# Moments of x ahead in six groups, routing of two chunks at once, and POOL's norms in front of rows and lists, in a fused cross-attention, time-mix and mixture-of-experts block

## What is computed

```python
x = x + cross_attention(layernorm(x), ctx, ctx)      # softmax over 257 context rows and the row's own sequence
h = layernorm(x)                                     # input of the second block
# second block: time mix, a scan over the 32 positions of a sequence, then experts
k, v, r = mix(ln1(h)) @ Wk, mix(ln1(h)) @ Wv, sigmoid(mix(ln1(h)) @ Wr)
y  = h + (r * wkv(k, v)) @ Wo
ei = ln2(y)
w, idx = top_2(softmax(ei @ router_w))               # 8 experts
moe = sum over the 2 experts of w * sigmoid(xr @ eWr) * (relu(xk @ eWk)**2 @ eWv)
x = x + y + moe
x = x + ffn(layernorm(x))                            # shared GEGLU and top-1 of 8 GEGLU experts
```

## Time and profile before

| | us |
|---|---|
| median of 3 runs | 963.76 (962.78 to 968.17) |
| the profiled execution | 966.43 |
| its span, first to last instruction | 964.7 |
| PE busy in the span | 858.3 |
| DVE busy | 445.0 |
| ACT busy | 316.3 |
| POOL busy | 349.3 |

### The profile page before, as it was taken

One profiled execution on the slowest core, in us unless ns is written; L12 is line 12 of the kernel. 1 busy time (PEld: TensorE's weight loads), 2 busy tenths in 40 slices (PEclk: granted clock), 3 DMA queues, 4 the chain that ended last, 5 costly groups with the idle time before them and its releaser, 6 DMA issues. The chain is left out here.

```text
span 964.7 us, 19179 instructions
## 1 busy us (share of the span) xinstructions
PE 858.3 (89%) x6306; PEld 768.6 (80%) x6306; DVE 445.0 (46%) x1253; ACT 316.3 (33%) x712; POOL 349.3 (36%) x605
## 2 busy tenths in 40 slices
PE   5899989886667999999949999968999999999994
PEld 4567766665566889999849999957999999999993
DVE  1279989888774555555523333353111111111113
ACT  1466767664542445555411111100111111111110
POOL 1445677766775355544142222211100010000006
PEclk9899999998688989999979999989999999999998
DMA  9875557534612322263121111102998988999716
GB/s 355 277 268 189 194 112 233 155 103 188 169 43 53 79 67 83 83 214 84 50 66 33 34 38 40 38 28 73 336 330 305 329 301 324 303 319 306 270 61 175
DMA packets 92096, 161.79 MB, mean 168 GB/s; under 512 B 13832, under 2 KB 71112, under 8 KB 88680
## 3 DMA queue, kind: packets, MB, share of 16 engines
q1 hardware_dynamic: 71008, 103.39, 32.2%
q10 hardware_dynamic: 12832, 37.82, 10.5%
q0 software_dynamic: 8176, 19.57, 7.9%
HBM read 146.10 MB, written 14.66 MB: 167 GB/s over the span
## 5 line engine op out<-in xcount | busy, mean ns | idle before, releaser
L1691 PEld LDWEIGHTS bank<-zT_f,we 128*128 128x128 f32 x1472 | 167.9, 192 | 1.8 <-ACT zT_f L1979 0.7
L1691 PE MATMUL bank<-zT_f,we 128*128 128x128 f32 x1472 | 168.2, 275 | 0.5 <-ACT zT_f L1979 0.5
L1708 DVE TENSOR_TENSOR hT_f<-bank,act_g 128x512 f32<-128x512 f32 x78 | 53.8, 691 | 227.6 <-PE bank L1691 208.0
L1700 ACT ACTIVATE act_g<-bank 128x512 f32<-128x512 f32 x78 | 46.6, 597 | 320.4 <-PE bank L1691 320.4
L1691 PE MATMUL bank<-zT_c,a_x 128*128 128x128 f32 x1024 | 121.4, 281 | 0.3 <-PEq L1521 0.3
L1691 PEld LDWEIGHTS bank<-zT_c,a_x 128*128 128x128 f32 x1024 | 119.2, 197 | 0.8 <-issue 0.7
L361 POOL DMA_INDIRECT arena_a<-rows_e,pick x78 | 76.0, 975 | 29.8 <-issue 29.8
L410 PE MATMUL bank<-arena_b,arena_a 128*128 128x128 f32 x624 | 81.8, 288 | 1.6 <-DVE hT L546 1.6
L1715 PE MATMUL bank<-we,hT_f 128*128 128x256 f32 x368 | 83.2, 379 | 0.0
L410 PEld LDWEIGHTS bank<-arena_b,arena_a 128*128 128x128 f32 x624 | 78.2, 204 | 2.4 <-DVE arena_b L538 2.4
L1715 PEld LDWEIGHTS bank<-we,hT_f 128*128 128x128 f32 x368 | 68.1, 190 | 8.3
(11 more groups left out here) (273 smaller groups left out, 1361.8 us busy)
## 6 DMA issues: line engine op xcount, KB each, us to landing
we<-in_W_dram SPq DMA_DIRECT2D x69, 1024.0 KB, 7.4
arena_a<-in_ctx_n_dram ACTq DMA_DIRECT2D x16, 1152.0 KB, 7.2
arena_a<-in_ctx_t_dram SPq DMA_DIRECT2D x16, 1028.0 KB, 9.0
rows_y<-arena_a ACTq DMA_DIRECT2D x39, 128.0 KB, 1.7
arena_a<-in_w_moe_dram ACTq DMA_DIRECT2D x3, 1156.0 KB, 5.3
arena_a<-in_w_moe_dram ACTq DMA_DIRECT2D x3, 1152.0 KB, 7.5
rows_f<-yr ACTq DMA_DIRECT2D x23, 128.0 KB, 6.3
rows_e<-arena_b SPq DMA_DIRECT2D x64, 32.0 KB, 4.0
```

The source lines that it names most:

```text
L1691: last = nc.tensor.matmul(bank[half][:, f * P:(f + 1) * P], w12[:, i, k, col0:col0 + P], zT[:, k], start=k == 0, stop=k == KD - 1)
L1700: nc.scalar.activation(act_g[:, half], bU[half][:], ACT.Gelu).then_inc(self.ac_g, 1)
L1708: nc.vector.tensor_tensor(hT[:, parity, half * HH:(half + 1) * HH].rearrange("p f t -> p (f t)"), bG[half][:], act_g[:, half], ALU.mult).t ...
```

## The change

DVE takes the moments of x in six groups instead of chunk by chunk: chunk 0 and chunk 1 at the start, then chunks 2 to 3 at the end of s = 0, 4 to 7 at the end of s = 2, 8 to 11 of s = 4, 12 to 15 of s = 5. POOL's `rstd0` treats a group with four instructions, and stands behind the step's other work and ahead of the constants. The last two loads of x are issued at s = 2 and s = 3, behind the keys; the zero rows and the zero table go out at s = 3. `time_mix_constants` is split: the part that waits for ACT runs at s = 2. Routing from `one_hot` to `slots` is done for two chunks in odd steps; `largest` and `largest_at` stay for each chunk, later in DVE's step; `both` stands behind one more drain; `own_rank` and `slots` come last. DVE's `attended` moves ahead of `moments1`. POOL's step is now numerator, with_bias, rstd3, rstd1, normed, lists, count, rstd0. Each list is written one step later, but 6 and 7 at s = 16 and 14 and 15 at s = 24.

```diff
+        M_PARTS = ((0, 1), (1, 2), (2, 4), (4, 8), (8, 12), (12, 16))
+        MOMENTS_AT = {0: 2, 2: 3, 4: 4, 5: 5}
 # mix_sync
-                if n in (5, 8):
-                    load_x(3 if n == 5 else 4)
                 if n < G:
                     load_keys(n)
-                if s == 2:
+                if s in (2, 3):
+                    load_x(s + 1)
+                if s == 3:
                     sp.wait_ge(po_mix, 1)
 # mix_pool
+            def decay_constants():
+                pool.wait_ge(ld_y, 16 * 2)
+                pool.wait_ge(wneg_done, 1)
                 nc.gpsimd.tensor_tensor(e_room[:], wexp[:], u_c, ALU.subtract)
...
+            def rstd0(i):
+                lo, hi = M_PARTS[i]
+                v, r, m = (rs0[:, j, lo:hi] for j in range(3))
+                pool.wait_ge(dv_st0, i + 1)
+                nc.gpsimd.tensor_scalar(v, mv0[:, lo:hi, 1], EPS, None, ALU.add).then_inc(po_v0, 1)
+                pool.wait_ge(po_v0, i + 1)
+                nc.gpsimd.tensor_tensor(r, v, eps_pow[:].to_broadcast([P, hi - lo]), ALU.pow).then_inc(po_p0, 1)
+                pool.wait_ge(po_p0, i + 1)
+                nc.gpsimd.tensor_scalar(m, mv0[:, lo:hi, 0], -1.0, None, ALU.mult).then_inc(po_n0, 1)
+                pool.wait_ge(po_n0, i + 1)
+                nc.gpsimd.tensor_tensor(m, m, r, ALU.mult).then_inc(po_r0, 1)
...
+            def count(q):
...
+                nc.gpsimd.tensor_tensor(earlier[:, 2], earlier[:, q % 2], mask[:, 0], ALU.add).then_inc(po_sum, 1)
+                pool.wait_ge(po_sum, 2 * q + 1)
+                nc.gpsimd.tensor_tensor(earlier[:, (q + 1) % 2], earlier[:, 2], mask[:, 1], ALU.add).then_inc(po_sum, 1)
...
+            def listed_at(i):
+                at_once = (CUT - 1, G - 1)
+                if i % 2:
+                    return (i - 1, i) if i in at_once else (i - 1,)
+                return () if i - 1 in at_once or i == 0 else (i - 1,)
...
-                if live(s + 1) is not None:
-                    rstd0(s + 1)
+                if s == 0:
+                    rstd0(1)
                 if w is not None:
                     numerator(w)
-                if i is not None:
-                    list_tokens(i)
-                if g is not None:
-                    normed(g)
-                if h is not None:
-                    count(h)
                 if a is not None:
                     with_bias(a)
                 if x is not None:
                     rstd3(x)
                 if c is not None:
                     rstd1(c)
+                if g is not None:
+                    normed(g)
+                if i is not None:
+                    for n in listed_at(i):
+                        list_tokens(n)
+                if h is not None and h % 2:
+                    count(h // 2)
+                if s in MOMENTS_AT:
+                    rstd0(MOMENTS_AT[s])
                 if s == 1:
                     time_mix_constants()
                 if s == 2:
+                    decay_constants()
                     routing_constants()
 # mix_tensor
+            def ranks(q):
+                pe.wait_ge(dv_mask, q + 1)
+                need(pe, po_sum, 2 * q)
+                need(pe, dv_prod, q)
+                upto(dv_dk, pe, 2 * q + 6)
+                two, odd = bK[:, D:D + 2 * E], bK[:, D + E:D + 2 * E]
+                nc.tensor.matmul(two, before_m[:], mask[:].rearrange("p c e -> p (c e)"), start=True, stop=False)
+                nc.tensor.matmul(bK[:, D:D + E], ones_m[:], earlier[:, q % 2], start=False, stop=False)
+                nc.tensor.matmul(odd, ones_m[:], earlier[:, q % 2], start=False, stop=False)
+                nc.tensor.matmul(odd, ones_m[:], mask[:, 0], start=False, stop=True).then_inc(pe_rank, 1)
...
-                if h is not None:
-                    ranks(h)
+                if h == CUT:
+                    totals_a()
+                if h is not None and h % 2:
+                    ranks(h // 2)
 # mix_vector
+            def stats0(i):
+                lo, hi = M_PARTS[i]
+                dve.wait_ge(ld_x[[a <= lo < b for a, b in X_PARTS].index(True)], 16)
+                for n in range(lo, hi):
+                    nc.vector.bn_stats(st0[:, n % 4], xz[:, n])
+                dve.drain()
+                for n in range(lo, hi):
+                    last = nc.vector.bn_aggr(mv0[:, n], st0[:, n % 4])
+                last.then_inc(dv_st0, 1)
...
                 if w is not None:
                     new_value(w)
                     denominator(w)
-                dve.drain()
                 if h is not None:
-                    one_hot(h)
+                    largest(h)
+                dve.drain()
+                if h is not None:
+                    largest_at(h)
                 if k is not None:
                     running_max(k)
                 dve.drain()
-                if h is not None:
-                    both(h)
+                if q is not None:
+                    one_hot(q)
...
                 dve.drain()
+                if q is not None:
+                    both(q)
                 if x is not None:
                     stats3(x)
...
                 if c is not None:
                     stats1(c)
-                if h is not None:
-                    sum_rank(h)
+                if b is not None:
+                    attended(b)
                 dve.drain()
                 if c is not None:
                     moments1(c)
-                if h is not None:
-                    slots(h)
-                if b is not None:
-                    attended(b)
...
+                if q is not None:
+                    own_rank(q)
+                dve.drain()
+                if q is not None:
+                    sum_rank()
                 if z is not None:
                     mixed(z)
+                if q is not None:
+                    dve.drain()
+                    slots(q)
                 if h == CUT:
                     tile_map_a()
                 if a is not None:
                     largest_score(a)
+                if s in MOMENTS_AT:
+                    stats0(MOMENTS_AT[s])
```

More of the change, by code:

```diff
@@ L166, in perceiver_block @@
         mask = sb("mask", [P, 2, E], BF16)
-        earlier = sb("earlier", [P, 2, E], BF16)
-        hot_rank = sb("hot_rank", [P, 2, E])
-        rank = sb("rank", [P, 2])
+        earlier = sb("earlier", [P, 3, E], BF16)
+        hot_rank = sb("hot_rank", [P, 2, 2, E])
+        rank = sb("rank", [P, 2, 2])
         token = sb("token", [P, G, 2], I32)
@@ L1293, in largest_at, with one_hot, both, own_rank @@
                 nc.vector.max_index(top_at[:, n % 2], top[:, n], logits[:, n])
-            def one_hot(n):
-                nc.vector.tensor_tensor(hot[:, n], iota_e[:].unsqueeze(1).to_broadcast([P, 2, E]),
-                                        top_at[:, n % 2, 0:2].unsqueeze(2).to_broadcast([P, 2, E]), ALU.is_equal)
-            def both(n):
-                need(dve, pe_rank, n - 1)
-                need(dve, po_sum, n - 1)
-                nc.vector.tensor_tensor(mask[:, n % 2], hot[:, n, 0], hot[:, n, 1], ALU.add).then_inc(dv_mask, 1)
-            def own_rank(n):
-                dve.wait_ge(pe_rank, n + 1)
-                nc.vector.tensor_tensor(hot_rank[:], hot[:, n], bK[:, D:D + E].unsqueeze(1).to_broadcast([P, 2, E]),
+            def one_hot(q):
+                nc.vector.tensor_tensor(hot[:, 2 * q:2 * q + 2], iota_e[:].unsqueeze(1).unsqueeze(1).to_broadcast([P, 2, 2, E]),
+                                        top_at[:, :, 0:2].unsqueeze(3).to_broadcast([P, 2, 2, E]), ALU.is_equal)
+            def both(q):
+                need(dve, pe_rank, q)
+                need(dve, po_sum, 2 * q)
+                two = hot[:, 2 * q:2 * q + 2]
+                nc.vector.tensor_tensor(mask[:], two[:, :, 0], two[:, :, 1], ALU.add).then_inc(dv_mask, 1)
+            def own_rank(q):
+                dve.wait_ge(pe_rank, q + 1)
+                ranks = bK[:, D:D + 2 * E].rearrange("p (c e) -> p c e", e=E)
+                nc.vector.tensor_tensor(hot_rank[:], hot[:, 2 * q:2 * q + 2], ranks.unsqueeze(2).to_broadcast([P, 2, 2, E]),
                                         ALU.mult).then_inc(dv_prod, 1)
-            def sum_rank(n):
+            def sum_rank():
                 nc.vector.reduce_sum(rank[:], hot_rank[:], AX)
-            def slots(n):
-                nc.vector.scalar_tensor_tensor(listed[:, n], top_at[:, n % 2, 0:2], float(TOK), rank[:],
+            def slots(q):
+                nc.vector.scalar_tensor_tensor(listed[:, 2 * q:2 * q + 2], top_at[:, :, 0:2], float(TOK), rank[:],
                                                ALU.mult, ALU.add).then_inc(dv_slot, 1)
@@ L1384, in mix_vector @@
             for s in range(STEPS):
[L1385 removed]
+                a, b, c = live(s), live(s - 1), live(s - 2)
+                if s == 0:
+                    stats0(1)
                 z, k, w, x, h = (live(s - LAG - i) for i in (0, 1, 2, 3, 5))
```

(7 more changed lines are left out.)

74 lines of the change are left out of this document (22 added, 52 removed).

## The result

The changed kernel takes 974.46 us (median of 6 runs, 973.41 to 976.19), the kernel before 965.92 beside it (6 runs). The ratio is 1.0093, 95% interval 1.0071 to 1.0114: slower by 0.9%. The forecast was 964.5 us and the range ended at 971.5, so it was wrong. 2.2 us of the miss are the base: the forecast stood on a median of 963.76 from three runs, and with three more it is 965.92. On that base the forecast would be 966.6 and the range would end at 973.7, still under the time measured. The profiled execution has a span of 972.3 us against 964.7.

A forecast was written before the change was run, and what follows sets the result against it. DVE and PE were taken as both full at s=9. Terms 3.0 - 0.8 - 10.5 - 0.5 + 5.2 + 4.3 + 0 gave +0.7 us: 967.1 against the profiled execution, 964.5 against the median; range 955.5 to 971.5.

The forecast's parts named there:

- Moments ahead: DVE's grouped moments at the end of s=4 and s=5 find no idle time there: +3.0 us.
- Steps 7, 8: At s=7 and s=8 PE takes over at once as what sets the step: -0.8 us.
- Routing: Routing two chunks at once on DVE: 12.07 us in even and 12.62 in odd steps, hardly a gain from pairing itself.
- Steps 9 to 15: Logit waits go and each step takes 12.5 us, POOL's adds costing nothing beyond: -10.5 us (-12.3 to -7).
- PE's path of 12.33: Steady-step loop from moments through POOL's norm, ACT, PE and attended back to the moments: 12.33 us a step.
- The rival: Slower through collisions: POOL's two adds beside DVE's two scans, 2 x 0.36 in nine steps, +6.5 us, 971; chance 0.08.
- POOL at s=2: Norm of group 3 waits for DVE's moments ahead of POOL's constants, po_set comes at 53.4: +5.2 us (4.5 to 6).
- s=18, +4.3: Late normed(10) delays stores, pick and gather(0), so DVE's quotient waits for POOL's numerator: +4.3 us (3.5 to 5).
- s=16, forecast -0.5: Term for step s=16 of the loop, a gain of 0.5 us.
- SP 0: Later loads of x and zero stores on SP make nothing wait: 0, at most +1 us.
- steps 19 to 24 0.0: Later mask delays PE's ranks in s=19, 21, 23 (+1.3, +0.3, +0.2); s=20 and 22 gain (-0.5, -1.3): together 0.0.
- The weighed rule: DVE instructions with two SBUF inputs and POOL instructions exclude each other; a collision costs 0.36 us, left out of the sum.

The follow-up runs named there:

- e11: Kernel before with only the moments of x in six groups, group norms behind POOL's constants; 966.82 us, ratio 0.9992.
- e12: Kernel before with only the routing in pairs of chunks, POOL's order as before; 958.09 us, ratio 0.9907.
- e13: Kernel before with only POOL's order changed: with_bias and the norms ahead of normed, lists and count; 970.78 us, ratio 1.0045.
- e9: Changed kernel with POOL's order in a step back: lists, normed and count ahead of with_bias and the norms; 967.21 us, ratio 1.0010.
- e4: Changed kernel with POOL's list DMAs ahead of normed's two adds; 971.35 us, single run.
- e10: The kernel of e8 with POOL's normed directly behind with_bias, ahead of the norms; 957.50 us, ratio 0.9893.
- e3: Changed kernel with SP issuing the nine picks at s=17 ahead of the stores of chunk 10; 971.21 us, ratio 1.0067.
- e8: The kernel of e7 with e3's edit and POOL's first two gathers behind numerator(13); 958.49 us, ratio 0.9919.
- e7: Changed kernel with attended back behind moments1, po_set's five memsets first on POOL at s=2, decay constants back at s=1; 968.47 us, ratio 1.0011.

## Why the prediction was wrong

Measured against the profiled execution, the sum said +0.7 and the span says +7.6, so 6.9 us are missing: 4.1 in steps 9 to 15, 1.8 at s=3, 0.9 of a later start, the rest in small terms. By its terms:

- *Moments ahead, +3.0*: measured +2.3. *Steps 7, 8*: -1.0 (-0.8). Right, and e11 shows that groups by themselves gain nothing.
- *Routing, "hardly a gain from pairing itself"*: wrong as a statement, harmless in the sum. e12 gains 6.1 us in steps 9 to 15 and 3.2 at the end. I had counted the end of the logit waits under POOL's order. `largest` asked for later is part of the routing edit and takes them away by itself (e12), and so does POOL's order (e13).
- *Steps 9 to 15, -10.5*: measured -6.4. **This is the step that failed**, in its last clause, that POOL's adds "cost nothing beyond the 12.5". Undisturbed steps did come out as worked out. An even step is 12.05 (e9; forecast 12.07). An odd step has 0.79 more: 0.19 for one_hot (e9), and by start-to-start differences between odd and even steps 0.15 for mask and 0.20 and 0.25 for the rank instructions with their drain; 12.84 (forecast 12.62). 3 x 12.05 + 4 x 12.84 = 87.5, the 7 x 12.5 of the forecast. That the two agree is in part luck: the odd step was put 0.22 too low, and the 0.12 a step that I had added for PE's path of 12.33 made up for it, while PE in fact waits for DVE (3.1 us at L901) and not the other way. The collisions are the rest: 7 x 0.32 for the scan, 4 x 0.37 for the one_hot (558 - 192 ns), 7 x 0.05 for the gate (465 - 416), 4.1 in sum, and 87.5 + 4.1 = 91.6 of 91.66. The rival gave each 0.36, the right size, but to both scans in nine steps, where only the first is hit, and 0.08 as its chance; that the numerator would hold the one_hot it didn't see. Unlike the sum suggests, the 4.1 can't simply be had back: e4, e9 and e10 took 0.1, 1.2 and 1.9 off the kernel that each was made from, the rest turned into other collisions or a wait for PE.
- *POOL at s=2, +5.2*: measured +7.0. Place, chain, po_set (53.4; 54.5 less the 0.9 of the later start) and the cost of the stop itself (5.3) were right. Missing was half clock on PE behind the stop, 1.7 us.
- *s=18, +4.3*: measured +4.7; s=16, forecast -0.5, gained nothing (s=16 and 17 are 27.25 us together, before and after). The mechanism is shown by e3 (picks), e9 and e13 (order) and e8 (gathers). But the comparison was too narrow: against the same kernel with POOL's old order (e9) the new order costs 6.6 at the end, as the routing would have gained there.
- *SP 0, steps 19 to 24 0.0*: -0.4 for the latter, with s=19 at +1.4 (forecast +1.3). Right in size; which instruction costs it there was not looked at. The start's 0.9 is no part of the change.

The weighed rule: scan 0.69 to 1.05 with two SBUF inputs beside POOL's add, L1276 and L1270, each with one operand from PSUM, unstretched at 0.42 and 0.40 beside the same adds, and the one_hot, 0.19 by itself, held until the numerator had ended. The Trainium skill, page SBUF — State Buffer, section "SBUF: two separate sides", lets a DVE instruction with two SBUF inputs and a GpSimd instruction that reads SBUF exclude each other for the whole instruction. The rows agree to about 0.1 us: at s=13 POOL's add ends at 177.49 and the scan, 0.69 by itself, at 178.04; the numerator ends at 181.06 and the one_hot at 181.14. It deserved a term in the sum and not a chance of 0.08.

## What to carry to other kernels

Where an engine is full, every place that another engine's work is moved to has a neighbour: list, for each moved instruction, what runs beside it and whether both read two SBUF operands, and price that in the sum. Ahead of a signal, put nothing that itself waits; the five memsets here came 6 us later, for a norm and constants placed in front of them, and the step lost 7.0 with PE's half clock behind it. And try the parts of a change alone: one of three carried all of the gain (e12, 0.9% faster than before), and single gains in a step that is nearly full don't add.

## What was not expected of the hardware

PE's granted clock at s=4 was 0.86 in one trace and 1.00 in another of the same instructions (e7, e8), worth 1.6 us. A 128x32 comparison of 0.19 us took 0.63 beside a 128x256 add of POOL of 0.74: what it pays is what is left of the neighbour, and not a share of its own length.
